# A fused attention, recurrence and expert layer: gates by b2 as one product, b1 sorted on the chip, weight pieces issued in a row

## What is computed

```
x = x + cross_attention(layernorm(x), context)        # 2048 keys a batch, 16 heads
x = x + recurrence(layernorm(x))                      # quantised products, scan over tokens, gated MLP
x = x + experts(x)                                    # top 2 of 8 experts
```

```
logits = xt @ Wr + br;  top_vals, top_idx = top_k(logits, 2)
gate = softmax(where(chosen, logits, -inf))           # two gates a token, 0 for the other six
h = relu(einsum('td,edh->teh', xt, W1) + b1)          # 8 experts, 2048 hidden
y = einsum('teh,ehd->ted', h, W2) + b2
out = einsum('ted,te->td', y, gate)                   # so b2 enters as gate @ b2
```

## Time and profile before

| | us |
|---|---|
| median of 3 runs | 1083.12 |
| the profiled execution | 1084.19 |
| its span in the trace | 1082.5 |
| TensorE (PE) busy | 1008.6 (93%) |
| VectorE (DVE) busy | 551.8 |
| ScalarE (ACT) busy | 434.6 |
| POOL busy | 256.4 |

### The profile page before, as it was taken

One profiled execution on the slowest core, in us unless ns is written; L12 is line 12 of the kernel. 1 busy time (PEld: TensorE's weight loads), 2 busy tenths in 40 slices (PEclk: granted clock), 3 DMA queues, 4 the chain that ended last, 5 costly groups with the idle time before them and its releaser, 6 DMA issues.

```text
span 1082.5 us, 17707 instructions
## 1 busy us (share of the span) xinstructions
PE 1008.6 (93%) x7135; PEld 787.2 (73%) x7142; DVE 551.8 (51%) x1147; ACT 434.6 (40%) x565; POOL 256.4 (24%) x221
## 2 busy tenths in 40 slices
PE   7899999999999998999999999757879999999996
PEld 6488777887677886777888776433459999977773
DVE  4334985465885456885454983587841111211110
ACT  3111786161776164686151785367611101111110
POOL 0301840001830000740001830696200101100000
PEclk9899999999999999999999999888959999999998
DMA  7183871523861514771431854600059978799700
GB/s 272 39 144 78 191 175 45 197 78 97 186 150 54 246 40 140 175 184 45 148 103 39 197 111 136 251 1 1 30 187 385 374 283 301 270 350 308 242 11 13
DMA packets 77899, 169.87 MB, mean 157 GB/s; under 512 B 7560, under 2 KB 17800, under 8 KB 72944
## 3 DMA queue, kind: packets, MB, share of 16 engines
q1 hardware_dynamic: 75696, 163.84, 49.7%
q0 software_dynamic: 2112, 4.80, 2.0%
HBM read 118.97 MB, written 16.10 MB: 125 GB/s over the span
## 4 chain that ended last, share of the span: by engine, by line
PE 77%; DVE 6%; DMA 4%; POOL 4%; issue 4%; ACT 3%; SPq 1%; DVEq 0%; POOLq 0%; ACTq 0%
PE psum L2071 11%; PE psum L455 8%; PE psum L435 7%; PE psum L2101 6%; PE psum L470 5%; PE psum L2086 5%; PE psum L374 5%; PE psum L391 5%; PE psum L392 5%; PE psum L393 5%; PE psum L375 5%; PE psum L376 5%; DMA ctx_raw<-in_ctx_t 2%; PE psum L423 1%; PE psum L1190 1%
## 5 line engine op out<-in xcount | busy, mean ns | idle before, releaser
L876 POOL CAST stack<-kT 128x2048 fp32r<-128x2048 f32 x32 | 63.2, 1981 | 410.5 <-ACT kT L752 397.5
L622 DVE CUSTOM_DVE_ANT_0 prob<-psum,biasmap,top 128x512 f32<-128x512 f32 x192 | 144.2, 751 | 23.4 <-PE psum L435 14.4
L790 ACT ACTIVATE prob<-prob,top 128x2048 f32<-128x2048 f32 x64 | 128.5, 2008 | 36.2 <-DVE top L622 36.0
L455 PE MATMUL psum<-ident,prob 128*128 128x128 f32 x1024 | 134.8, 274 | 7.1 <-ACT probT L798 4.3
L455 PEld LDWEIGHTS psum<-ident,prob 128*128 128x128 f32 x1024 | 116.2, 141 | 27.9 <-issue 12.4
L2071 PE MATMUL psum<-xT,wring 128*128 128x128 f32 (+3 forms) x1024 | 134.2, 292 | 0.6 <-ACT xT L2332 0.6
L2071 PEld LDWEIGHTS psum<-xT,wring 128*128 128x128 f32 x1024 | 132.1, 193 | 2.8 <-issue 1.9
L798 ACT COPY probT<-psum 128x1024 f32<-128x1024 f32 x96 | 96.6, 1011 | 51.7 <-PE psum L470 50.0
L752 ACT COPY kT<-psum 128x512 f32<-128x512 f32 x64 | 37.6, 587 | 197.7 <-PE psum L376 191.8
L2260 DVE TENSOR_SCALAR hidden<-psum,b 128x128 f32<-128x128 f32 (+3 forms) x64 | 23.7, 370 | 162.6 <-PE psum L2071 162.5
L391 PE MATMUL psum<-wv_hi,ctx_part 128*128 128x512 f32 x256 | 100.6, 393 | 0.0
(11 more groups left out here) (241 smaller groups left out, 1550.9 us busy)
## 6 DMA issues: line engine op xcount, KB each, us to landing
wring<-in_w SPq DMA_DIRECT2D x64, 1024.0 KB, 9.7
ctx_raw<-in_ctx_t SPq DMA_DIRECT2D x15, 1024.0 KB, 5.8
stack<-stack SPq DMA_DIRECT2D x32, 256.0 KB, 4.7
early_stack<-early_stack SPq DMA_DIRECT2D x28, 256.0 KB, 5.0
ternary<-ternary_weights SPq DMA_DIRECT2D x1, 6272.0 KB, 24.5
prob<-in_w_gate_t SPq DMA_DIRECT2D x1, 5632.0 KB, 17.4
stack<-key_stack SPq DMA_DIRECT2D x20, 256.0 KB, 4.0
query_stacks<-prob SPq DMA_DIRECT2D x16, 256.0 KB, 5.4
```

The lines of the kernel that those rows point to most:

```text
L455: mm = pe.transpose(psum[:, w + i, j * P:(j + 1) * P], prob[:, prob_slot(n, j), kt * P:(kt + 1) * P], ident[:, :])
L622: dve.tensor_tensor_reduce(prob[:, slot, keys], psum[:, scores.of[n, j, c], :], biasmap[:, keys], 1.0, top[:, h, (c + 1) % 2:(c + 1) % 2 + ...
L790: act.activation(prob[:, slot, :], prob[:, slot, :], ACT.Exp, bias=top[:, h, 1:2], scale=-1.0, accum_out=top[:, h, 2:3]).then_inc(*raised. ...
```

## The change

Three parts, of which the first has work in two stages.

*Gates by b2.* b2 is loaded three times, at partitions 0, 32 and 64 of `b2_raw` (96 partitions, cleared by POOL before), rounded to float32r by POOL into `b2_stack`, and the rows from 64 on are replaced by the rest (raw less rounded). The gates are laid out in the same way (high, rest, high) in `gate_stack`. One float32r product with 96 rows a batch then gives high x high + rest x high + high x rest. `gateT` has 96 partitions. The first two sums are added to x1 before the jobs, the other two inside job 0, after `gate_slots(0)`.

*b1.* It is loaded whole during the recurrence. POOL multiplies it by `same` (128 x 1024 elements) and VectorE reduces over e, which gives b1 in rank order. ScalarE and VectorE wait for that before job 0.

*Issue.* The eight small DMAs between weight pieces 0 and 1 are gone. The four products for `place_at` become one instruction.

```diff
+            def clear_stacks():
+                pool.wait_ge(*x1_added.at(B - 1))
+                pool.memset(b2_raw[:, :], 0.0).then_inc(*constants.made("b2_cleared"))
             def router_constants():
-                pool.wait_ge(*x1_added.at(B - 1))
+                pool.wait_ge(*route_in.at("b2", GATE_AT[-1]))
+                pool.tensor_copy(b2_stack[:, :], b2_raw[:, :]).then_inc(*own.made())
+                pool.wait_ge(*own.last())
+                low = slice(GATE_AT[2], GATE_AT[2] + EXPERTS)
+                pool.tensor_tensor(b2_stack[low, :], b2_raw[low, :], b2_stack[low, :].bitcast(F32), ALU.subtract).then_inc(*own.made())
+                pool.wait_ge(*own.last())
+                pool.memset(gate_stack[:, :, :].bitcast(F32), 0.0)
...
             keep_residual(3)
+            clear_stacks()
             spread_quantum(3)
...
-            sp.dma_start(b2[:, :], a["b2"]).then_inc(*route_in.made("b2"))
+            sp.dma_start(b1_all[:, :, :], a["b1_t"]).then_inc(*route_in.made("b1"))
+            sp.wait_ge(*constants.at("b2_cleared"))
+            for at in GATE_AT:
+                sp.dma_start(b2_raw[at:at + EXPERTS, :], a["b2"]).then_inc(*route_in.made("b2", at))
...
-                pe.matmul(psum[:, w, :], gateT[:, b * P:(b + 1) * P], b2[:, :], start=True,
+                pe.matmul(psum[:, w, :], gateT[:, b * P:(b + 1) * P], b2_stack[:, :], start=True,
                           stop=True).then_inc(*routed_t.made("b2", b))
...
-            for b in tokens:
-                spread_out_places = dve.tensor_tensor(
-                    place_at[:, b, :, :], same[:, :, :],
-                    place[:, b:b + 1, :].broadcast_to([P, EXPERTS, EXPERTS]), ALU.mult)
-            spread_out_places.then_inc(*own.made())
+            dve.wait_ge(*routed_v.at("same"))
+            dve.tensor_tensor(place_at[:, :, :, :], ..., ALU.mult).then_inc(*own.made())
...
+                    if q == 0:
+                        add_b2(2)
+                        add_b2(3)
                     if q + 1 < end:
                         mark_picks(q + 1)
...
+            parts = [gate_stack[:, :, at:at + EXPERTS] for at in GATE_AT]
+            dve.tensor_copy(parts[0], gate[:, :, :]).then_inc(*own.made())
+            dve.tensor_copy(parts[2], gate[:, :, :])
+            dve.wait_ge(*own.last())
+            dve.tensor_tensor(parts[1], gate[:, :, :], parts[0].bitcast(F32),
+                              ALU.subtract).then_inc(*routed_v.made("gate"))
...
+            dve.wait_ge(*b1_marked.at("all"))
+            dve.tensor_reduce(b1[:, :, :].rearrange("p r h -> p (r h)"),
+                              b1_at[:, :, :, :].rearrange("p r h e -> p (r h) e"), AX.X,
+                              ALU.add).then_inc(*routed_v.made("b1"))
+            add_b2(0)
+            add_b2(1)
...
+            pool.wait_ge(*routed_v.at("same"))
+            pool.tensor_tensor(b1_at[:, :, :, :], b1_all..., same..., ALU.mult).then_inc(*b1_marked.made("all"))
             pool.wait_ge(*rows_out.at("meta"))
             jobs(0, MAIN)
...
                     load_piece(q, i, at)
-                    if (q, i) == (0, 0):
-                        for r in range(EXPERTS):
-                            sp.dma_start(b1[:, r, :], a["b1_t"][:, bass.ds(expert_at(r), 1), :].rearrange(
-                                "p e h -> p (e h)")).then_inc(*b1_in.made(r))
```

More of the change, by code:

```diff
@@ L211, in perceiver_block @@
             Steps(sem(name)) for name in ("tensor_own", "vector_own", "scalar_own", "gpsimd_own"))
-        constants = events("constants", ["ident", "all", "bias", "zeros", "integer_ident", "router"])
+        constants = events("constants", ["ident", "all", "bias", "zeros", "integer_ident", "b2_cleared", "router"])
         wv_in, wq_in, bias_in = (events(name, ["all"], 16) for name in ("wv_in", "wq_in", "bias_in"))
@@ L1012, in perceiver_block @@
         region_2 = ExitStack()
+        GATE_AT, STACKED = (0, 32, 64), 96
         rows_f = sb("work", [P, B, D], F32, region_2)
@@ L1033, in perceiver_block @@
         br = sb("br", [P, EXPERTS], F32, region_2)
-        b2 = sb("b2", [EXPERTS, D], F32, region_2)
+        b1_all = sb("b1_all", [P, EXPERTS, HT], F32, region_2)
+        b2_raw = sb("b2_raw", [STACKED, D], F32, region_2)
+        b2_stack = sb("b2_stack", [STACKED, D], F32R, region_2)
+        gate_stack = sb("gate_stack", [P, B, STACKED], F32R, region_2)
         iota_e = sb("iota_e", [P, EXPERTS], F32, region_2)
@@ L1066, in perceiver_block @@
         small_in = events("small_in", ["attn_norm", "g_norm", "mlp_norm", "lower"], 16)
-        route_in = events("router_in", ["wr", "br", "b2"], 16)
+        route_in = events("router_in", ["wr", "br", "b1", *(("b2", at) for at in GATE_AT)], 16)
         QUANTISED = (("a", 0), ("a", 1), ("a", 2), ("a", 3), ("o", 0), ("o", 1), ("m", 0), ("o", 2), ("m", 1),
@@ L1222, in route @@
                 if b == 0:
-                    pe.wait_ge(*route_in.at("b2"))
+                    pe.wait_ge(*route_in.at("b2", GATE_AT[-1]))
                 pe.wait_ge(*x2_copied.at(b))
@@ L1937, in perceiver_block @@
         b1 = sb("b1", [P, EXPERTS, HT], F32)
+        b1_at = sb("b1_at", [P, EXPERTS, HT, EXPERTS], F32)
         apart = sb("apart", [P, B, 2], F32)
@@ L1941, in perceiver_block @@
         gate_second = sb("gate_second", [P, B, EXPERTS], F32)
-        gateT = sb("gateT", [EXPERTS, B * P], F32)
+        gateT = sb("gateT", [STACKED, B * P], F32R)
         chosen = sb("chosen", [P, B, EXPERTS], BF16)
@@ L1972, in wide @@
             return JOBS[q][2] > P
-        b1_in = events("b1_in", range(EXPERTS), 16)
-        routed_v = events("routed_v", ["apart", "chosen", "meta", "order", "gate", "load",
+        b1_marked = events("b1_marked", ["all"])
+        routed_v = events("routed_v", ["apart", "chosen", "meta", "order", "same", "gate", "load", "b1",
                                        *(("out", b) for b in tokens)])
@@ L2007, in perceiver_block @@
         TURN_AT, ID_AT = 2, 5
-        b2_banks = ((y_banks, 4), (y_banks, 5), (hidden_banks, 0), (hidden_banks, 1))
+        b2_banks = ((hidden_banks, 0), (hidden_banks, 1), (y_banks, 4), (y_banks, 5))
         def last_tile(q):
@@ L2138, in tensor_experts @@
             for b in tokens:
-                mm = pe.transpose(psum[0:EXPERTS, 2, b * P:(b + 1) * P], gate[:, b, :], ident[:, :])
+                mm = pe.transpose(psum[0:STACKED, 2, b * P:(b + 1) * P], gate_stack[:, b, :].bitcast(F32), ident[:, :])
             mm.then_inc(*routed_t.made("gatesT"))
@@ L2202, in vector_experts @@
                               iota_e[:, :].rearrange("p (o e) -> p o e", o=1).broadcast_to([P, EXPERTS, EXPERTS]),
-                              ALU.is_equal).then_inc(*own.made())
+                              ALU.is_equal).then_inc(*routed_v.made("same"))
             dve.wait_ge(*own.last())
-            for b in tokens:
-                spread_out_places = dve.tensor_tensor(
-                    place_at[:, b, :, :], same[:, :, :],
-                    place[:, b:b + 1, :].broadcast_to([P, EXPERTS, EXPERTS]), ALU.mult)
-            spread_out_places.then_inc(*own.made())
+            dve.wait_ge(*routed_v.at("same"))
+            dve.tensor_tensor(place_at[:, :, :, :],
+                              same[:, :, :].rearrange("p (o r) e -> p o r e", o=1).broadcast_to(
+                                  [P, B, EXPERTS, EXPERTS]),
+                              place[:, :, :].rearrange("p b (o e) -> p b o e", o=1).broadcast_to(
+                                  [P, B, EXPERTS, EXPERTS]), ALU.mult).then_inc(*own.made())
             dve.wait_ge(*own.last())
@@ L2274, in gate_output, with add_b2 @@
                                   slot_gate[0:count, q % 2, st, 2:3], None, ALU.mult).then_inc(*y_ready_v.made(q))
+            def add_b2(b):
+                dve.wait_ge(*routed_t.at("b2", b))
+                dve.tensor_tensor(x1[:, b, :], psum[:, b2_banks[b][0].of["b2", b], :], x1[:, b, :],
+                                  ALU.add).then_inc(*routed_v.made("out", b))
             def jobs(first, end):
@@ L2301, in vector_experts @@
             dve.wait_ge(*own.last())
-            dve.tensor_tensor(gate[:, :, :], gate[:, :, :], gate_second[:, :, :],
-                              ALU.add).then_inc(*routed_v.made("gate"))
+            dve.tensor_tensor(gate[:, :, :], gate[:, :, :], gate_second[:, :, :], ALU.add).then_inc(*own.made())
+            dve.wait_ge(*own.last())
+            dve.wait_ge(*constants.at("router"))
+            parts = [gate_stack[:, :, at:at + EXPERTS] for at in GATE_AT]
+            dve.tensor_copy(parts[0], gate[:, :, :]).then_inc(*own.made())
+            dve.tensor_copy(parts[2], gate[:, :, :])
+            dve.wait_ge(*own.last())
+            dve.tensor_tensor(parts[1], gate[:, :, :], parts[0].bitcast(F32),
+                              ALU.subtract).then_inc(*routed_v.made("gate"))
```

(15 more changed lines are left out.)

## The result

| | before | after |
|---|---|---|
| median | 1080.38 us (8 runs) | 1085.72 us (8 runs, 1084.9 to 1089.7) |
| ratio | | 1.0054, 95% interval 1.0035 to 1.0072 |
| profiled execution | 1084.19 | 1089.70 |
| its span | 1082.5 | 1088.0 |

The changed kernel is slower by 0.5%, some 5.8 us of 1080 with an interval of 3.8 to 7.8. The span of the profiled executions grew by 5.5 us. It splits at two marks, the start of `same` on VectorE (L2200, now L2220) and the first hidden product on TensorE (L2071, now L2091).

What follows compares the result with a forecast made beforehand. Bounds taken: POOL at two places in the recurrence, TensorE's b2 product at the router's end. Clear 0.5, constants 2.4 and router 1.4 sum to +4.3 us on the median 1083.12: 1087.5 us, range 1081.5 to 1092.

Steps and rivals of the forecast that it cites:

- no change that can be told: Whole kernel: a measured difference within 5.4 us (0.5%) either way, given chance 0.65.
- the sum had 2.9: Recurrence, ahead of the router: 0.5 us for the clear and 2.4 us for the router's constants, both charged in full.
- Clear, 0.5: POOL memset of b2_raw after keep_residual(3): 0.53 us, charged in full as +0.5; bounds 0 and 0.6.
- Constants, 2.4: Three POOL instructions before root_gained(2): +2.4 us, charged in full because other engines wait for the root; bounds 1.0 and 3.0.
- The marks are held: Router: VectorE's marks stand still until POOL's b1 multiplication ends; row numbers and gather come 1.55 us later.
- VectorE is there first: Router, after same: VectorE runs place_at first, so POOL's b1 multiplication starts only when place_at ends, at 792.1.
- The price I put beside it, 0.6: Router: if POOL won the race, place_at would be held as well, adding some 0.6 us to the sum.
- The gather under load, 6.2: Router: with the weight stream full, the second gather takes 6.18 us from issue to end, against 3.1; bounds 3.1 and 7.5.
- The rival that the queues share fairly: Router: DMA queues served in turn, the gather keeps its 3.1 us; total +1.2, 1084.3 us; chance 0.10.
- The product's saving is unseen: End of router: the float32r b2 product saves TensorE over 4 us, yet unseen because the gather ends last.
- The 3.2 us that the prediction gave as exposed: End of router: about 3.2 us of b2's old product lies beyond the gather's landing, the most this part can give.
- The clock: Experts on TensorE start at 1.2 GHz; each us longer or shorter there is worth half a us; only widens the range.

Runs made afterwards that it cites:

- e7: Changed kernel with router constants, clear, POOL's b1 multiplication, weight pieces 1 to 7 and the waits for b1 all moved; 0.9952 of the kernel before, -5.2 us.
- e8: Changed kernel with b1 by eight small DMAs as before, router constants and clear moved, waits for b1 later; 0.9945 of the kernel before, -5.9 us.
- e1: Changed kernel with POOL's multiplication of b1 moved behind the two gather instructions of job 0; 1.0029 of the kernel before, +3.1 us.
- e2: Changed kernel with POOL's multiplication of b1 released by the end of place_at, not by same; 1.0046 of the kernel before, +5.0 us.
- e3: Changed kernel with weight pieces 1 to 7 of job 0 issued only after its gather has landed; 1.0030 of the kernel before, +3.2 us.
- e6: Changed kernel with b1 as before (eight small DMAs between weight pieces 0 and 1), stacks and float32r product kept; 0.9992 of the kernel before, -0.9 us.

## Why the prediction was right, and where a step was not

The forecast was +4.3 us (1087.5); measured are +5.3 by the medians and +5.8 by the ratio. The time itself, 1085.72, is 1.8 below the forecast, because the kernel before has a median of 1080.38 over eight runs where the forecast was built on 1083.12 over three. The largest chance, 0.65, lay on no change that can be told, with 5.4 us as the bound; what was measured lies about at this bound, and the interval excludes zero. Ahead of the router the sum had 2.9 and the profile shows 2.64; in the router it had 1.4 and the profile shows 2.20; the experts' 0.66 it did not have.

That 2.64 lies so near 2.9 is in part luck. Its parts are -0.64 ahead of keep_residual(3), where POOL's program is the same, +0.42 from there to join_residual(1), +0.22 to join_residual(2) and +2.64 to same. The two that belong to the change make 3.06, and the other two, which differ from one execution to the next, happen to take 0.42 back.

*Clear, 0.5.* Right in size: the memset took 0.52 us. From keep_residual(3) to join_residual(0) the stage took 18.02 us where it took 17.27, and the next one 9.37 for 9.70: net 0.4. With the clear moved (e7, e8) the first is 17.26 again.

*Constants, 2.4.* Right: 2.47, each of the three instructions within 0.04 of its term, and all of it on the path. From join_residual(2) to the last normalise it was 41.06 us before and is 43.94: nothing of it was made up by then.

*The marks are held.* The mechanism was right and its place was wrong. "VectorE is there first" failed. Before, place_at started 0.03 us after same had ended; in the changed kernel, where VectorE has one more wait in front of it, it starts 0.10 after (e1 shows this without POOL), and POOL starts 0.08 after. So POOL was first and place_at was held. It ended 0.28 us after POOL's product, and the row numbers lost 2.45 us and not 1.55. About half of the missing 0.9 is the order: with the assumed one (e2) they come 0.43 earlier. Most of the rest is a term that was mis-sized: POOL's product took 2.76 and not the 2.4 worked out from flat operands. The sentence of the Trainium skill, "SBUF — State Buffer", section "SBUF: two separate sides", that an op with two SBUF inputs is held too and that the first one has the ports, is what the runs show (3.02 against 0.42). The price I put beside it, 0.6, was somewhat too high for the order alone, which cost 0.43.

*The gather under load, 6.2.* Right: 6.05, and 3.04 without the stream (e3). The rival that the queues share fairly is out. It rested on a sentence of the Trainium skill, "DMA: Bandwidth & Descriptors", section "Queues, rings and completion order", that a DMA engine serves its queues in turn, packet by packet; no run here shows the order of service, and what fails is my conclusion from it that the gather keeps its 3.1 us. It ends 3 us later with the same packets (2112 in the software queue in either run).

*The product's saving is unseen.* Right: 5.1 us were saved on TensorE and it waited 4.3 us for the gather. The 3.2 us that the prediction gave as exposed was close: with a gather of 3.4 (e6) it is 2.9.

*The clock* was in the range and not in the sum, and that was right: the 0.66 us of the last stretch lie within what executions differ by there.

## What to carry to other kernels

Before giving an idle-looking engine a constant to prepare, look at who waits for that engine at that very place; the same instructions cost 2.5 us ahead of one root and about 1 us in POOL's next long wait. A release of two engines by one event is a race: if one of them is then a long POOL operation and the other is on the path, put POOL's behind the last thing that the path needs from POOL (e1: the marks end 2.6 us earlier). To let only the path's first instruction go ahead, by its own event, gained 0.4 us here (e2), because the next ones were held in its place. And a transfer on which the path waits should be issued into an empty queue: bulk loads with slack are better held until it has landed.

## What the hardware did that I had not expected

The recurrence is not one time. From join_residual(1) to join_residual(2) all kernels here run the same instructions, and their profiled executions took 6.97 to 9.60 us. TensorE's clock goes between its two levels in this stage, at different places in each execution: from join_residual(0) to join_residual(1) its mean was 0.50 in the changed kernel and 0.82 in e2, and in the stage after that 0.96 and 1.00. The changed kernel and e2 have the same instructions in the whole recurrence; from join_residual(0) to join_residual(2) they show:

```profile
724.92:743.13 18.21, 13.24 (x53) 6.12 (x53) 13.96 (x36) 13.44 (x30) 14.84 (x24) 0.72 0.00 0
```

```profile
721.46:737.81 16.35, 11.07 (x53) 5.39 (x53) 14.13 (x36) 13.40 (x30) 14.81 (x23) 0.90 0.00 1
```

The columns are those of the earlier trace rows. The first row (the changed kernel) has a mean granted clock of 0.72 and TensorE busy for 13.24 us, the second (e2) 0.90 and 11.07, with 53 matmul records in both; the stretch took 18.21 and 16.35 us. This stage is not the largest part of how executions differ. POOL's first L1765, near the start of the recurrence, starts at 681.25 us in the changed kernel and at 676.66 in e3, with the same instructions up to there: 4.6 us arise ahead of it, and why was not tried. The eight executions of the changed kernel lie 4.8 us apart. It is why differences of 1 to 2 us are read from stages of the trace here, and the ratios only say whether they are there. And a stage of the trace is one execution: only a difference that returns in several kernels is safe, as the 18.0 us from keep_residual(3) to join_residual(0) does, found in every kernel with the clear in its first place, against 17.3 in every other.
